# A selective scan in steps of a chunk pair: products of 1024 columns, all products with C on GpSimd, scan result in PSUM

## The chip, the cores and the metric

One core of a Trainium2 chip runs the whole program in one launch. Its engines are TensorE (PE), VectorE (DVE), ScalarE (ACT), GpSimd (POOL) and the queue of SyncE (SP), which issues the transfers. The metric is the device time of one execution in microseconds, from three runs.

## The reference

The input is 16 sequences of 512 positions and 256 channels. A bidirectional selective state-space layer, a residual and a layer norm come first, then a soft mixture of 16 experts with 64 slots each, a residual and a last layer norm. The change touches the scan of the state-space layer alone. For each direction, each of 512 inner channels and each of 16 states n the reference computes, along the positions:

```
dA      = dt * A[n];   dB_u = dt * u * B[n]
dA_cum  = exp(sum of dA over the later positions)
xs      = cumsum(dB_u * dA_cum) / (dA_cum + 1e-12)
y      += xs * C[n]
```

The kernel computes xs as a linear recurrence, s = e * s + g with e = exp(A dt) and g = dt u B, times a guard factor that stands for the 1e-12: (1 + tanh(...)) / 2, with the half folded into C.

## The kernel before, in words

The program has three stages: `sequence_stage` (a loop over the 16 sequences, a prologue and an epilogue), `expert_stage` and `merge_stage`. Only the first is touched.

The 512 inner channels are four chunks of 128 partitions. The scan of a sequence is cut into 128 tiles: two directions, two chunk pairs, 16 states, and the two chunks of the pair (`dir_of`, `chunk_of`, `state_of`). A tile is one state of one chunk, 128 partitions by 512 positions. `TILES` is 128, and a run of 32 tiles (`SEG`) accumulates one pair of chunks of y in PSUM. For a tile t the work is:

- SP (L366, in `load`) broadcasts the rows of B and C for a state to all partitions, into `b_ring` and `c_ring`, three buffers each; one row serves both chunks of a pair.
- ACT (L616, `decay`) writes e into `e_ps`, two banks of PSUM, and (L630) tanh into `f_ps`, two banks of PSUM. e of tile t+1 comes before f of tile t, and must wait for the scan of tile t-1.
- POOL (L504, `inputs`) writes g = dtu * B into `g_ring`, two tiles ahead.
- DVE (L808, `scan`) scans e and g into `s_ring` in SBUF; (L816, `guard`) multiplies (1 + f) by s. For an even tile the result goes back into bank 0 of `f_ps`, and DVE itself multiplies it by C (L825, `times_c`). For an odd tile it goes into `z_ring` in SBUF, and POOL multiplies it by C (L513). Both products go into `v_ring`, six tiles.
- PE (L963) adds v into `y_ps` by a product with the identity, two turns behind; L967 adds the skip term.

DVE's order is: guard(t), scan(t+1), C product of t if t is even. So between a scan and the guard that reads it there is other work, and nothing waits for the instruction just before it.

All engines run the same unrolled 128 tiles per sequence, each in its own program order. Between the tiles each does its share of side work: the projections, convolutions, softplus, norms, softmax over rows and columns and slots of neighbouring sequences. `timetable` and `slot_tiles` fix the tile of each of the side pieces; a piece is filled by PE at its tile and handled by ACT and DVE two to nine tiles later (`side_step`). The two banks of `side` hold the pieces in turn. The two layer norms are split into 15 small steps each, two to a tile, from tile 14 to tile 28 (`norms`, `norm_part`, `norm_step`; the small lines are L64 to L75, the last is L78). Side work on DVE that appears in the rows is L704 (conv gate), L699 (residual gate), L714, L717, L721, L726 and L737 (softplus and the suffix sum of dt), L757 (column softmax), L779 and L785 (copying y out and gating it). POOL also makes dtu = dt * u (L483).

Of the kernel before, what the change touches and what calls it, by code (L numbers as in the profile page):

```python
# [23 lines left out]
P = 128  # L24
# [106 lines left out]
def sequence_stage(nc, xT, x, in_wT, conv_w, conv_b, x_wT, dt_wT, dt_b, A_log, D, out_wT,  # L131
# [28 lines left out]
    TILES = NDIR * PAIRS * SEG  # L160
    assert L == 512 and KI == 4 and KM == 2 and LT == 4 and S == 2 * HS and N == 16
# [13 lines left out]
    VR = 6  # L175


    RING = [i % 3 for i in range(TILES // 2)]
    RING[-1] = 1

# [7 lines left out]
    def dir_of(t):  # L188
        return t // (PAIRS * SEG)
# [4 lines left out]
    with ExitStack() as ctx:  # L194
# [8 lines left out]
        f_ps = ctx.enter_context(nc.psum_tensor("f_ps", [P, 2, 512], F32))  # L203
# [70 lines left out]
        f_ready, g_done, scan_done, z_done = sem("f_ready"), sem("g_done"), sem("scan_done"), sem("z_done")  # L274
        v_even, v_odd, v_used = sem("v_even"), sem("v_odd"), sem("v_used")
# [49 lines left out]
        def _(sp):  # L325
# [25 lines left out]
            def load(at, i, c):  # L351
# [3 lines left out]

                last = max(j for j in range(i - TILES // 2, i) if RING[j % (TILES // 2)] == RING[i])
                if c == 0:
                    sp.wait_ge(g_done, at.b * TILES + (2 * last + 2 + CR))
                else:
                    sp.wait_ge(v_even, at.b * (TILES // 2) + (last + 1 + CR))  # L360
                    sp.wait_ge(v_odd, at.b * (TILES // 2) + (last + 1 + CR))
# [58 lines left out]
            def steps(at, load_next_x):  # L420
                load(at, 0, 0)
                for i in range(TILES // 2):
                    if i + 1 < TILES // 2:
                        load(at, i + 1, 0)
# [47 lines left out]
        def _(pool):  # L472
            make_identity(pool, ident, ident_done)
            pool.sem_inc(v_odd, CR)
# [14 lines left out]
            with pool.Fori(0, B, 1) as b:  # L489
                at = At("loop", b, pool)  # L490
                t0 = pool.snap(b * TILES)
                t0_half = pool.snap(b * (TILES // 2))

                def inputs(t):

                    d, c, i = dir_of(t), chunk_of(t), t // 2
                    if t % (TILES // NDIR) == 0:
                        pool.wait_ge(dtu_done, b * 8 + (d + 1) * KI)
                    k = RING[i]

                    loaded = (b_loaded if t % 2 == 0 else c_loaded)[k]
                    pool.wait_ge(loaded, b * (RING.count(k) * 16) + (RING[:i].count(k) + 1) * 16)
                    pool.wait_ge(scan_done, t0 + (t - 3 + CR))
                    pool.tensor_tensor(g_ring[:, t % 4], dtu[d][:, c], b_ring[:, k], ALU.mult).then_inc(g_done, 1)  # L504

                inputs(0)
                inputs(1)
                for t in range(TILES):
                    if t + 2 < TILES:
                        inputs(t + 2)  # L510
                    if t % 2 == 1:
                        pool.wait_ge(z_done, t0 + (t + 1 + CR))
                        pool.tensor_tensor(v_ring[:, t % VR], z_ring[:, t // 2 % 3], c_ring[:, RING[t // 2]],  # L513
                                           ALU.mult).then_inc(v_odd, 1)
                    for lag in (8, 9):
                        for s in slots_at(t - lag, ("dt0", "dt1")):
                            if TABLE[s][1] % 2 == 1:
                                dtu_of_pair(at, s, (TABLE[s][1] - 9 + lag,))
# [3 lines left out]
        def _(act):  # L522
# [81 lines left out]
            with act.Fori(0, B, 1) as b:  # L604
                at = At("loop", b, act)
                t0 = act.snap(b * TILES)
                t0_half = act.snap(b * (TILES // 2))
                seq4 = act.snap(b * 4)

                def decay(t):  # L610
# [5 lines left out]
                    act.activation(e_ps[:, t % 2], dt[d][:, c], ACT.Exp, scale=a_neg[:, d, c, n:n + 1])  # L616

                decay(0)
                for t in range(TILES):
                    d, c, n = dir_of(t), chunk_of(t), state_of(t)  # L620
                    if t + 1 < TILES:
                        decay(t + 1)
                    if t % (TILES // NDIR) == 0:
                        act.wait_ge(rsum_done, b * 8 + (d + 1) * KI)

                    if t % 2 == 0:
                        act.wait_ge(v_even, t0_half + (t // 2 + CR))
                    else:
                        act.wait_ge(z_done, t0 + (t - 1 + CR))
                    act.activation(f_ps[:, t % 2], rsum[d][:, c], ACT.Tanh,  # L630
                                   scale=a_neg_half[:, d, c, n:n + 1], bias=guard_bias[:]).then_inc(f_ready, 1)
                    for s in range(SLOTS):
                        side_step(at, s, t - tile_of[s])
# [7 lines left out]
        def _(dve):  # L641
# [8 lines left out]
            for sem_, n in ((side_free[0], CR), (side_free[1], CR), (scan_done, CR), (z_done, CR), (v_even, CR),  # L650
# [140 lines left out]
            with dve.Fori(0, B, 1) as b:  # L791
                at = At("loop", b, dve)
                t0 = dve.snap(b * TILES)

# [5 lines left out]
                def scan(t):  # L800

                    flip = (lambda ap: ap) if dir_of(t) == 0 else (lambda ap: ap[:, ::-1])

                    dve.wait_ge(f_ready, t0 + max(t, 1))
                    dve.wait_ge(g_done, t0 + (t + 1 + CR))
                    if t == 0:
                        dve.wait_ge(z_done, t0 + CR)
# [464 lines left out]
```

## Time and profile before

| what | value |
|---|---|
| runs | 7026.24 us median of three (7024.77 to 7026.32) |
| profiled execution, span from first to last instruction | 7017.1 us |
| what the median of the runs has beyond that span | 9.1 us |
| sequence loop within the span | 92.7 to 5934.5 us |
| busy: PE, DVE, ACT, POOL | 78%, 82%, 60%, 60% |
| granted TensorE clock, mean | 0.885 |

For the profiled execution there is no time but its span; the runs were timed by themselves. Busy shares are over the whole span, in which the last 1080 us or so hold no work for POOL. A mean of durations mixes instructions that ran freely with those that were held by something while they ran. The columns of each view are told with its first group of rows below.

### The profile page before, as it was taken

What the parts mean: (1) busy time and instruction counts of PE and PEld (TensorE: products, weight loads), DVE (VectorE), ACT (ScalarE), POOL (GpSimd) and SP (SyncE); (2) the same over time, 40 slices, a digit from 0 to 9 for tenths busy, and PEclk for the clock granted to TensorE, in tenths of its full rate; (3) what the DMA queues carried; (4) which work ended last, traced back from release to release, by engine and by line L of the source; (5) the groups of instructions that cost most, each with busy time, mean ns of one, the idle gap of its engine ahead of it and who ended that gap; (6) DMA issues with size and microseconds to landing.
All of it is one profiled execution on the core that took longest, in us unless ns stands there. A gap on an engine that the chain in (4) does not pass through costs nothing. (4 is left out here: it accounts for less than half of the span.)

```text
span 7017.1 us, 79490 instructions
## 1 busy us (share of the span) xinstructions
PE 5452.5 (78%) x14584; PEld 2611.9 (37%) x14584; DVE 5767.6 (82%) x8375; ACT 4186.0 (60%) x6495; POOL 4206.1 (60%) x3210
## 2 busy tenths in 40 slices
PE   5777777777777777878786877777777777899978
PEld 2333333333333333333333333333333333556566
DVE  7999999989999999999999999999999998222223
ACT  4767676666767676767676767676767665211100
POOL 3767777777777776767676767676777775000000
PEclk8988888888888888889898989898988898999989
DMA  2333333333333333333342423333333332322355
GB/s 76 115 99 113 102 111 102 109 103 107 106 104 105 107 103 110 108 99 116 95 121 90 122 91 119 94 115 99 114 100 112 102 109 79 93 87 87 92 187 203
DMA packets 554755, 755.05 MB, mean 108 GB/s; under 512 B 123584, under 2 KB 272064, under 8 KB 552192
## 3 DMA queue, kind: packets, MB, share of 16 engines
q1 hardware_dynamic: 554240, 750.73, 34.7%
q14 instruction: 503, 4.12, 0.2%
q8 instruction: 12, 0.20, 0.0%
HBM read 660.80 MB, written 89.75 MB: 107 GB/s over the span
## 5 line engine op out<-in xcount | busy, mean ns | idle before, releaser
L963 PE MATMUL y_ps<-v_ring,ident 128*128 128x512 f32 x4096 | 2388.9, 689 | 858.9 <-POOL v_ring L513 304.3
L504 POOL TENSOR_TENSOR g_ring<-dtu,b_ring 128x512 f32<-128x512 f32 x2048 | 2726.3, 1350 | 40.1 <-DMA b_ring<-bc_scr 27.5
L808 DVE TENSOR_TENSOR_SCAN s_ring<-e_ps,g_ring 128x512 f32<-128x512 f32 x2048 | 2478.8, 1210 | 80.8 <-POOL g_ring L504 80.8
L513 POOL TENSOR_TENSOR v_ring<-z_ring,c_ring 128x512 f32<-128x512 f32 x1024 | 1296.1, 1266 | 1599.3 <-DVE z_ring L816 1599.2
L616 ACT ACTIVATE e_ps<-dt,a_neg 128x512 f32<-128x512 f32 x2048 | 1408.7, 688 | 1084.6 <-DVE s_ring L808 1078.6
L630 ACT ACTIVATE f_ps<-rsum,guard_bias,a_neg_half 128x512 f32<-128x512 f32 x2048 | 1572.0, 768 | 30.9 <-DVE z_ring L816 30.3
L963 PEld LDWEIGHTS y_ps<-v_ring,ident 128*128 128x128 f32 x4096 | 775.2, 212 | 2008.9 <-issue 881.3
L816 DVE SCALAR_TENSOR_TENSOR f_ps<-f_ps,s_ring 128x512 f32<-128x512 f32 x1024 | 707.6, 691 | 229.5 <-ACT f_ps L630 186.3
L816 DVE SCALAR_TENSOR_TENSOR z_ring<-f_ps,s_ring 128x512 f32<-128x512 f32 x1024 | 696.1, 680 | 92.3 <-ACT f_ps L630 92.2
L825 DVE TENSOR_TENSOR v_ring<-f_ps,c_ring 128x512 f32<-128x512 f32 x1024 | 679.1, 663 | 0.0
L896 PE MATMUL side<-u,conv_diag 128*128 128x512 f32 x1056 | 489.6, 607 | 41.6 <-ACT disp_ring L597 41.6
L1063 ACT ACTIVATE x_act<-x_gate,x_bg 128x512 f32<-128x512 f32 x128 | 87.9, 687 | 561.6 <-PE x_gate L1095 561.6
L1077 DVE SCALAR_TENSOR_TENSOR x_hT<-x_up,x_bu,x_act 128x512 f32<-128x512 f32 x128 | 96.2, 751 | 373.4 <-PE x_up L1099 373.4
L924 PE MATMUL side<-seT,xnT 128*128 128x512 f32 x544 | 288.8, 659 | 128.6 <-ACT xnT L565 97.6
L944 PE MATMUL side<-dispT_ring,xn 128*128 128x128 f32 x2176 | 299.3, 296 | 67.8 <-ACT dispT_ring L573 67.8
L944 PEld LDWEIGHTS side<-dispT_ring,xn 128*128 128x128 f32 x2176 | 292.5, 211 | 146.9 <-ACT dispT_ring L573 101.2
L896 PEld LDWEIGHTS side<-u,conv_diag 128*128 128x128 f32 x1056 | 203.3, 194 | 309.2 <-issue 254.4
L1207 PE MATMUL m_acc<-m_eo,m_pT 128*128 128x256 f32 x1024 | 240.9, 401 | 64.6 <-DMA m_rinv<-rinv_scr 64.6
L889 PE MATMUL side<-xT_t,w_in 128*128 128x512 f32 x528 | 281.4, 661 | 5.5 <-DVE a_neg L683 4.7
L483 POOL TENSOR_TENSOR dtu<-dt,u 128x512 f32<-128x512 f32 x132 | 233.4, 1769 | 81.2 <-DVE dt L726 81.2
L929 PE MATMUL side<-xnT,seT 128*128 128x512 f32 x544 | 276.4, 635 | 0.0
L1095 PE MATMUL x_gate<-x_xT,x_wg 128*128 128x512 f32 x512 | 242.5, 596 | 16.0 <-DMA x_bu<-in_bu 16.0
(123 smaller groups left out, 5728.4 us busy)
## 6 DMA issues: line engine op xcount, KB each, us to landing
b_ring<-bc_scr SPq DMA_DIRECT2D x1024, 256.0 KB, 3.2
c_ring<-bc_scr SPq DMA_DIRECT2D x1024, 256.0 KB, 3.2
pT_scr<-rowT_ring SPq DMA_DIRECT2D x136, 256.0 KB, 3.6
m_pT<-pT_scr SPq DMA_DIRECT2D x16, 2048.0 KB, 8.3
sT_scr<-sT_ring SPq DMA_DIRECT2D x272, 64.0 KB, 2.4
x_xT<-sT_scr SPq DMA_DIRECT2D x16, 1024.0 KB, 8.9
eo_scr<-x_eo SPq DMA_DIRECT2D x32, 512.0 KB, 5.1
m_eo<-eo_scr SPq DMA_DIRECT2D x16, 1024.0 KB, 10.8
```

Of the source, the lines that this page charges most:

```text
L504: pool.tensor_tensor(g_ring[:, t % 4], dtu[d][:, c], b_ring[:, k], ALU.mult).then_inc(g_done, 1)
L513: pool.tensor_tensor(v_ring[:, t % VR], z_ring[:, t // 2 % 3], c_ring[:, RING[t // 2]], ALU.mult).then_inc(v_odd, 1)
L616: act.activation(e_ps[:, t % 2], dt[d][:, c], ACT.Exp, scale=a_neg[:, d, c, n:n + 1])
L630: act.activation(f_ps[:, t % 2], rsum[d][:, c], ACT.Tanh, scale=a_neg_half[:, d, c, n:n + 1], bias=guard_bias[:]).then_inc(f_ready, 1)
L808: dve.tensor_tensor_scan(flip(s_ring[:, t % 3]), flip(e_ps[:, t % 2]), flip(g_ring[:, t % 4]), 0.0, ALU.mult, ALU.add).then_inc(scan_done, 1)
L816: dve.scalar_tensor_tensor(out=z, in0=f_ps[:, t % 2], scalar=1.0, in1=s_ring[:, t % 3], op0=ALU.add, op1=ALU.mult).then_inc(z_done, 1)
L825: dve.tensor_tensor(v_ring[:, t % VR], f_ps[:, 0], c_ring[:, RING[t // 2]], ALU.mult).then_inc(v_even, 1)
L889: mm = pe.matmul(bank, w_in[:, k, m * P:(m + 1) * P], xT_t[:, k], start=(k == 0), stop=(k == KM - 1))
L896: mm = pe.matmul(bank, conv_diag[:, d, i, k], src[:, i, k:k + L], start=(k == 0), stop=(k == KC - 1))
L924: mm = pe.matmul(bank, xnT[:, k, t * P:(t + 1) * P], seT[:, k, h * HS:(h + 1) * HS], start=(k == 0), stop=(k == KM - 1))
L944: mm = pe.matmul(bank[:, k * P:(k + 1) * P], xn[:, t, k * P:(k + 1) * P], dispT_ring[:, i % 2, t * P:(t + 1) * P], start=(t == 0), stop=(t ...
L963: pe.matmul(y_ps[:, t % 2], ident[:], v_ring[:, t % VR], start=(state_of(t) == 0), stop=True, skip_group_check=True).then_inc(v_used, 1)
```

## The change

What is done by tile becomes done by step, a step being the two tiles of one state of a chunk pair (`STEPS` = 64).

- POOL makes g for both chunks in one product of 1024 columns, the row of B broadcast over the two, into `g_ring` of three pairs, one step ahead. It also makes all products with C, one of 1024 columns a step, into `v_ring` of three pairs. C products on DVE are gone.
- The scan writes into PSUM (`s_ps`, two banks, in the place of `f_ps`); ACT writes tanh into SBUF (`f_ring`, two pairs).
- DVE makes one guard product of 1024 columns a step, into `z_ring` (two pairs in SBUF). Its order is scan(2i), scan(2i+1), guard(i). The guard waits for both scans, and the next scan waits for the guard, since it overwrites `s_ps`.
- ACT's f comes one tile earlier in its order, right behind e of the same tile, with a semaphore of its own for each.
- PE adds v five turns behind (`Y_LAG`) instead of two, and the skip terms go by PE's turn. y is copied out at the fourth tile of a run instead of the second, and gated one tile later.
- The scratch of the program for software-made transfers is set to 1024, which leaves SBUF for the larger rings.

```
-    VR = 6
+    FR, ZR = 2, 2
+    Y_LAG = 5
...
-        f_ps = ctx.enter_context(nc.psum_tensor("f_ps", [P, 2, 512], F32))
+        s_ps = ctx.enter_context(nc.psum_tensor("s_ps", [P, 2, 512], F32))
...
-        g_ring = sb("g_ring", [P, 4, L])
-        s_ring = sb("s_ring", [P, 3, L])
-        z_ring = sb("z_ring", [P, 3, L])
-        v_ring = sb("v_ring", [P, VR, L])
+        g_ring = sb("g_ring", [P, 3, 2, L])
+        f_ring = sb("f_ring", [P, FR, 2, L])
+        z_ring = sb("z_ring", [P, ZR, 2, L])
+        v_ring = sb("v_ring", [P, 3, 2, L])
...
+                def inputs(i):
...
+                    pool.wait_ge(scan_done, t0 + (2 * (before(i) + 1) + CR))
+                    pool.tensor_tensor(g_ring[:, RING[i]], dtu[d][:, pair:pair + 2], both(b_ring[:, k:k + 1]),
+                                       ALU.mult).then_inc(g_done, 1)
+                def times_c(i):
...
+                    pool.wait_ge(z_done, step0 + (i + 1 + CR))
+                    pool.wait_ge(v_used, t0 + (2 * (before(i) + 1) + CR))
+                    pool.tensor_tensor(v_ring[:, RING[i]], z_ring[:, i % ZR], both(c_ring[:, k:k + 1]),
+                                       ALU.mult).then_inc(v_done, 1)
...
+                for i in range(STEPS):
+                    if i + 1 < STEPS:
+                        inputs(i + 1)
+                    times_c(i)
...
+                def guard(t):
...
+                    if t % 2 == 0:
+                        act.wait_ge(z_done, step0 + (i - FR + 1 + CR))
+                    act.activation(f_ring[:, i % FR, t % 2], rsum[d][:, c], ACT.Tanh,
+                                   scale=a_neg_half[:, d, c, n:n + 1], bias=guard_bias[:]).then_inc(f_done, 1)
...
                 def scan(t):
...
+                    dve.wait_ge(e_done, t0 + (t + 1))
+                    if t % 2 == 0:
+                        dve.wait_ge(g_done, step0 + (i + 1 + CR))
+                        dve.wait_ge(z_done, step0 + (i + CR))
+                    dve.tensor_tensor_scan(flip(s_ps[:, t % 2]), flip(e_ps[:, t % 2]), flip(g_ring[:, RING[i], t % 2]), 0.0,
                                            ALU.mult, ALU.add).then_inc(scan_done, 1)
+                def guarded(i):
+
+                    dve.wait_ge(f_done, t0 + (2 * i + 2))
+                    dve.wait_ge(scan_done, t0 + (2 * i + 2 + CR))
+                    dve.wait_ge(v_done, step0 + (i - ZR + 1 + CR))
+                    dve.scalar_tensor_tensor(out=z_ring[:, i % ZR], in0=f_ring[:, i % FR], scalar=1.0, in1=s_ps[:],
                                              op0=ALU.add, op1=ALU.mult).then_inc(z_done, 1)
...
                 for t in range(TILES):
                     part = t // SEG
-                    if t % SEG == 2:
-                        dve.wait_ge(v_used, t0 + (t - 2 + CR))
+                    if t % SEG == 4:
+                        dve.wait_ge(v_used, t0 + (SEG * part + CR))
                         y_out(at, part)
-                    if t % SEG == 3 and part in (0, 3):
+                    if t % SEG == 5 and part in (0, 3):
                         y_gate(at, part)
+                    scan(t)
                     norms(t, 0)
-                    guard(t)
-                    if t + 1 < TILES:
-                        scan(t + 1)
-                    if t % 2 == 0:
-                        times_c(t)
+                    if t % 2 == 1:
+                        guarded(t // 2)
                     norms(t, 1)
...
-                for turn in range(TILES + 2):
-                    t = turn - 2
+                for turn in range(TILES + Y_LAG):
+                    t = turn - Y_LAG
```

## Rows read from the trace of the kernel before

**Rows 1.** Page, part 1: busy us (share of the span) and instructions by engine.

```profile
PE 5452.5 (78%) x14584; PEld 2611.9 (37%) x14584; DVE 5767.6 (82%) x8375; ACT 4186.0 (60%) x6495; POOL 4206.1 (60%) x3210
```

**Rows 2.** Windows: sequence loop; tiles 14-29, 32-39, 68-75 of one sequence.

```profile
core 0: us, PE busy (x) PEld busy (x) DVE busy (x) ACT busy (x) POOL busy (x), PEclk, DMA share, GB/s
92.72:5934.50 5841.78, 4446.09 (x11144) 1956.42 (x11145) 5429.77 (x7442) 4026.24 (x6252) 4195.66 (x3199) 0.87 0.35 106
3046.76:3100.72 53.96, 42.44 (x89) 15.84 (x87) 51.84 (x97) 31.03 (x48) 30.80 (x24) 0.94 0.28 83
3104.95:3128.91 23.96, 14.01 (x28) 5.01 (x27) 22.17 (x29) 17.97 (x25) 15.96 (x12) 0.78 0.33 102
3209.12:3226.06 16.94, 16.89 (x67) 9.56 (x66) 16.52 (x21) 14.94 (x26) 14.95 (x12) 1.00 0.49 149
```

**Rows 3.** Page, part 5: groups of instructions; busy, mean ns, idle before.

```profile
L504 POOL TENSOR_TENSOR g_ring<-dtu,b_ring 128x512 f32<-128x512 f32 x2048 | 2726.3, 1350 | 40.1 <-DMA b_ring<-bc_scr 27.5
...
L816 DVE SCALAR_TENSOR_TENSOR f_ps<-f_ps,s_ring 128x512 f32<-128x512 f32 x1024 | 707.6, 691 | 229.5 <-ACT f_ps L630 186.3
L816 DVE SCALAR_TENSOR_TENSOR z_ring<-f_ps,s_ring 128x512 f32<-128x512 f32 x1024 | 696.1, 680 | 92.3 <-ACT f_ps L630 92.2
L825 DVE TENSOR_TENSOR v_ring<-f_ps,c_ring 128x512 f32<-128x512 f32 x1024 | 679.1, 663 | 0.0
...
L483 POOL TENSOR_TENSOR dtu<-dt,u 128x512 f32<-128x512 f32 x132 | 233.4, 1769 | 81.2 <-DVE dt L726 81.2
```

**Rows 4.** Waits: who waited for whom, total us, times, longest.

```profile
POOL v_ring L513 <- DVE z_ring L816: 1599.2, 974, 4.0
...
DVE f_ps L816 <- ACT f_ps L630: 186.3, 128, 2.0
...
DVE z_ring L816 <- ACT f_ps L630: 92.2, 80, 1.9
```

**Rows 5.** Timeline of DVE in tiles 69 and 70: start, us, line, operation.

```profile
3211.05 1.21 DVE L808 TENSOR_TENSOR_SCAN s_ring<-e_ps,g_ring 128x512 f32<-128x512 f32 x1
3212.18 0.67 DVE L825 TENSOR_TENSOR v_ring<-f_ps,c_ring 128x512 f32<-128x512 f32 x1
3212.76 0.68 DVE L816 SCALAR_TENSOR_TENSOR z_ring<-f_ps,s_ring 128x512 f32<-128x512 f32 x1
3213.36 1.21 DVE L808 TENSOR_TENSOR_SCAN s_ring<-e_ps,g_ring 128x512 f32<-128x512 f32 x1
```

**Rows 6.** One line of the kernel: durations min/median/max in ns.

```profile
L779 DVE TENSOR_TENSOR yg<-y_ps,yg x33: 1199/1199/1224, 98.1 to 5928.7; 128x1024 f32<-128x1024 f32 x33
```

**Rows 7.** Timeline around 3055 us, all engines, in a tile with norm steps.

```profile
3054.64 1.27 POOL L513 TENSOR_TENSOR v_ring<-z_ring,c_ring 128x512 f32<-128x512 f32 x1 [4.00 <-DVE z_ring L816]
...
3055.61 0.33 DVE L66 TENSOR_SCALAR tmp<-mv 128x4 int32<-128x4 int32 x1
...
3055.86 1.27 POOL L504 TENSOR_TENSOR g_ring<-dtu,b_ring 128x512 f32<-128x512 f32 x1
3055.97 1.19 DVE L68 TENSOR_SCALAR rstd<-tmp 128x4 int32<-128x4 int32 x1
```

**Rows 8.** Five lines of DVE with two SBUF operands or more: durations min/median/max.

```profile
L71 DVE SCALAR_TENSOR_TENSOR tmp<-rstd x102: 146/306/1225, 140.3 to 5951.3; 128x4 f32<-128x4 f32 x102
...
L714 DVE TENSOR_SCALAR rsum<-dtu x132: 395/546/1245, 71.8 to 5902.6; 128x512 f32<-128x512 f32 x132
...
L737 DVE TENSOR_TENSOR_SCAN rsum<-one,dt x132: 1210/1366/2215, 77.4 to 5919.1; 128x511 f32<-128x511 f32 x132
...
L757 DVE TENSOR_SCALAR disp_ring<-disp_ring,col_inv x136: 471/576/1423, 240.1 to 6016.4; 128x512 f32<-128x512 f32 x136
...
L704 DVE SCALAR_TENSOR_TENSOR u<-dt,u x132: 675/680/823, 52.7 to 5826.4; 128x512 f32<-128x512 f32 x132
```

**Rows 9.** Timelines of DVE and POOL from 3000.2 us.

```profile
3000.38 2.19 DVE L737 TENSOR_TENSOR_SCAN rsum<-one,dt 128x511 f32<-128x511 f32 x1
...
3001.45 2.17 POOL L504 TENSOR_TENSOR g_ring<-dtu,b_ring 128x512 f32<-128x512 f32 x1
```

**Rows 10.** Timeline of DVE at the start of the ninth sequence.

```profile
3012.48 1.23 DVE L808 TENSOR_TENSOR_SCAN s_ring<-e_ps,g_ring 128x512 f32<-128x512 f32 x1 [5.10 <-POOL g_ring L504]
```

More of the change, by code:

```diff
@@ L173, in sequence_stage, with before @@
     CR = 256
-    VR = 6
-    RING = [i % 3 for i in range(TILES // 2)]
+    FR, ZR = 2, 2
+    Y_LAG = 5
+    RING = [i % 3 for i in range(STEPS)]
     RING[-1] = 1
+    def before(i):
+        return max(j for j in range(i - STEPS, i) if RING[j % STEPS] == RING[i])
     def slots_at(t, kinds):
@@ L354, in load @@
                 ring, loaded = ((b_ring, b_loaded), (c_ring, c_loaded))[c]
-                last = max(j for j in range(i - TILES // 2, i) if RING[j % (TILES // 2)] == RING[i])
+                last = before(i)
                 if c == 0:
-                    sp.wait_ge(g_done, at.b * TILES + (2 * last + 2 + CR))
+                    sp.wait_ge(g_done, at.b * STEPS + (last + 1 + CR))
                 else:
-                    sp.wait_ge(v_even, at.b * (TILES // 2) + (last + 1 + CR))
-                    sp.wait_ge(v_odd, at.b * (TILES // 2) + (last + 1 + CR))
+                    sp.wait_ge(v_done, at.b * STEPS + (last + 1 + CR))
                 if i % (PAIRS * N) == 0 and c == 0:
@@ L506, in _ @@
-                inputs(0)
[L507 to L518, printed above, removed]
+                step0 = pool.snap(b * STEPS)
@@ new lines, in both @@
+                def both(row):
+                    return row.broadcast_to([P, 2, L])
+                def inputs(i):
+                    d, pair, k = dir_of(2 * i), chunk_of(2 * i), RING[i]
+                    if i % (STEPS // NDIR) == 0:
+                        pool.wait_ge(dtu_done, b * 8 + (d + 1) * KI)
+                    pool.wait_ge(b_loaded[k], b * (RING.count(k) * 16) + (RING[:i].count(k) + 1) * 16)
+                    pool.wait_ge(scan_done, t0 + (2 * (before(i) + 1) + CR))
+                    pool.tensor_tensor(g_ring[:, RING[i]], dtu[d][:, pair:pair + 2], both(b_ring[:, k:k + 1]),
+                                       ALU.mult).then_inc(g_done, 1)
@@ L521, in _ @@
+                for i in range(STEPS):
+                    if i + 1 < STEPS:
+                        inputs(i + 1)
+                    times_c(i)
+                    for t in (2 * i, 2 * i + 1):
+                        for lag in (8, 9):
+                            for s in slots_at(t - lag, ("dt0", "dt1")):
+                                if TABLE[s][1] % 2 == 1:
+                                    dtu_of_pair(at, s, (TABLE[s][1] - 9 + lag,))
         @block.scalar
@@ L615, in decay @@
                     act.wait_ge(scan_done, t0 + (t - 1 + CR))
[L616 to L620, printed above, removed]
-                    if t + 1 < TILES:
-                        decay(t + 1)
+                    act.activation(e_ps[:, t % 2], dt[d][:, c], ACT.Exp, scale=a_neg[:, d, c, n:n + 1]).then_inc(e_done, 1)
+                def guard(t):
+                    d, c, n, i = dir_of(t), chunk_of(t), state_of(t), t // 2
                     if t % (TILES // NDIR) == 0:
@@ L626, in _ @@
                     if t % 2 == 0:
[L627 to L631, printed above, removed]
+                        act.wait_ge(z_done, step0 + (i - FR + 1 + CR))
+                    act.activation(f_ring[:, i % FR, t % 2], rsum[d][:, c], ACT.Tanh,
+                                   scale=a_neg_half[:, d, c, n:n + 1], bias=guard_bias[:]).then_inc(f_done, 1)
+                decay(0)
+                guard(0)
+                for t in range(TILES):
+                    if t + 1 < TILES:
+                        decay(t + 1)
+                        guard(t + 1)
                     for s in range(SLOTS):
@@ L649, in _ @@
             dve.memset(y_ps[:], 0.0).then_inc(init_done, 1)
-            for sem_, n in ((side_free[0], CR), (side_free[1], CR), (scan_done, CR), (z_done, CR), (v_even, CR),
+            for sem_, n in ((side_free[0], CR), (side_free[1], CR), (scan_done, CR), (z_done, CR),
                             (x1_done, CR), (xn_normed, CR), (rinv_done, CR)):
@@ L793, in _ @@
                 t0 = dve.snap(b * TILES)
+                step0 = dve.snap(b * STEPS)
                 def norms(t, j):
```

50 lines of the change are left out of this document (13 added, 37 removed).

## The prediction

> **What bounds the kernel now.** I read the page's totals first, then windows, then single instructions. The totals [rows 1] give VectorE (DVE) 82% and GpSimd (POOL) 60%. The sequence loop takes 5841.8 us of the span, or 365.1 per sequence, and in it DVE is busy 93% and POOL 72%; the code after it is not touched [rows 2]. The costliest groups [rows 3] are the scan work. The waits [rows 4] show the order: POOL waits 1599 us for DVE's z, while DVE waits only 186 + 92 = 279 us for ACT's f and hardly for POOL. DVE is the bound.
>
> A step is one state of one chunk pair: two scans, two guards and one C product on DVE, three products on POOL, 64 steps a sequence. In a step without other DVE work starts follow each other by 1.13 us (scan), 0.60 (guard) and 0.58 (C product), because an instruction that waits for nothing starts some 0.08 before the last one ends [rows 5]. That is 2 x 1.13 + 2 x 0.60 + 0.58 = 4.04, and the four steps of tiles 68 to 75 take 16.94 us, 4.24 each [rows 2]. Steps with side work take 6 to 8: the eight with the norms (tiles 14 to 29) take 53.96 together, the four of tiles 32 to 39 take 23.96 [rows 2].
>
> **What the change does to DVE.** The C product goes (0.58). Two guards become one of 1024 columns, which I price from a DVE product of 1024 with one input in PSUM, 1.20 (L779), plus the 0.02 by which the guard exceeds the C product at 512: 1.22 [rows 3, 6]; bounds 1.20 and 2 x 0.69. But the overlap is lost: guard(i) now waits for the scan just before it, and the next scan for guard(i). An instruction that waits for its predecessor starts about 0.035 after it (L66 ends 3055.94, L68 starts 3055.97) [rows 7]. A bare step is 1.13 + 1.21 + 0.035 + 1.22 + 0.035 = 3.63. So DVE is relieved of 0.41 a step, not of 0.66. The scan's output in PSUM I cost at nothing, since the guard into PSUM takes 691 ns against 680 into SBUF [rows 3]; the upper bound is 0.06 each, 0.12 a step, and nothing in these rows allows a gain.
>
> **What it does to POOL.** Per step two products of 1024 columns. No row has this size. Spacing of 512-column products back to back is 1.23 (L513 at 3054.64, L504 at 3055.86) [rows 7], so the upper bound is 2.47. If the fixed share were DVE's (C product 663 ns at 512, 1200 at 1024 [rows 3, 6]), it would be 1.26 x 1.81 = 2.28. I take 2.35, near the middle, and two are 4.70. That alone exceeds the 4.24 of a bare step today: POOL becomes the bound of every step without side work. The order on POOL is g(i+1), v(i), and v(i) waits for z(i), so it can't run ahead more than one step.
>
> The Trainium skill (GPSIMD Engine Reference, Performance versus the Vector engine) gives 4497 ns for a two-input product of 2048 columns. With the 1.26 us of the trace at 512 a line through both gives 2.34 at 1024; the sum would be the same.
>
> **The wait that grows.** Some DVE instructions stretch when POOL is in a product. L71 on four columns takes 146 ns at least and 1225 at most, L737 1210 to 2215, L714 395 to 1245, L757 471 to 1423 [rows 8]. The pair at 3055 shows how: L66 starts while v runs and ends at 3055.94, with v's end (3055.91); g has started at 3055.86, and L68, which waits for L66, ends at 3057.16, with g's end (3057.13) [rows 7]. So the DVE instruction waits until POOL's current product ends, POOL's next one gets in between, and a dependent second instruction waits for a whole product. The other way round POOL loses time too: the product at 3001.45 takes 2.17 while L737 of 1.21 runs its course, so it is held about 0.9, 0.3 less than the instruction's length [rows 9]. All that stretch have two inputs in SBUF, or one input and an output there; scans, guards and C products, with one operand in PSUM, don't.
>
> The Trainium skill (SBUF — State Buffer, Who interferes with whom) says that such a DVE instruction and GpSimd exclude each other for a whole instruction. The trace agrees (L66 and L68 above), and the rule speaks against this change: products twice as long, on an engine that hardly rests, mean longer waits. Without the rule only the faster rival below would stand.
>
> Per sequence there are, by their shortest durations [rows 8]: 8 each of L704 (0.68), L714 (0.40), L737 (1.21), L757 (0.47), and of L717 and L721, taken like L704; 4 of L699, the same; 4 of L726 and 2 of L785, 1024 columns, taken at 1.22 from L779 [rows 6]; 24 small ones of the norms (0.15, as L71) and 8 of L78 (0.40, as L714). Sum 50 us, of which 11 lie in the eight norm steps and 39 in others.
>
> **A step after.** A step begins with scan(2i) when g(i) is there or z(i-1) is done; at that moment v(i-1) starts, too. In a step with such an instruction behind the even scan: it arrives at 1.13, waits until 2.39 (v's end), ends at 2.26 + d, then 1.13 + 0.035 + 1.22 + 0.035: 4.68 + d. POOL has 4.70 + d - 0.3. Behind the guard it delays POOL or DVE by about its length. So 56 steps cost 4.70 each, 263.2, plus their 39 us: 302.2.
>
> Norm steps: in an even tile two dependent small instructions stand side by side. The first ends with v (2.41), POOL's g gets in, the second ends with g (4.74); then scan, guard and two small ones: 7.3. The steps are, with gate and conv instructions (0.6 each), statistics (4 x 0.32 + 0.6) and L78 (4 x 0.32): 6.1, 7.9, 7.9, 10.5, 6.7, 7.9, 7.3, 9.0, together 63.3 against 54.0 now.
>
> Rest: DVE work in PSUM that now finds no gap (row and column maxima, output copies) 5, the eight dtu products of 512 on POOL (1.24 each, half hidden) 4, two places with two such instructions in one tile 3: 12. End of a sequence: 5.1 idle now, until the first g of the next is there [rows 10]; the first g becomes 1.1 longer: 6.2. f in two buffers of a pair takes away DVE's 279 us of waits for ACT, 17 a sequence, which are in today's 365 and not in my sum. TensorE has 16.89 busy in the 16.94 us of tiles 68 to 75, at full granted clock [rows 2]: no spare at 4.24, some at 4.70. Y_LAG 5 gives a filled bank more lead, and v has two steps until its buffer is wanted again; nothing for these, nor for SP, whose loads stay in order and wait for work three steps back.
>
> Sum: 302.2 + 63.3 + 12 + 6.2 = 383.7 per sequence, 18.6 more than 365.1, times 16 is +298. The profiled span 7017.1 becomes 7315; the median of the runs is 9.1 above the span: 7324, say 7325.
>
> **Rivals.** (1) The waits fall into DVE's slack, and POOL's own sum decides: 64 x 4.70 + 10 dtu + 13 held (today (142 + 67) / 16, from the means of L504 and L483 over 1.26 [rows 3]) + 6.2 = 330, or 6470. For it: a bare step leaves DVE 1.07 free, and today the median of L704 is 680 ns against 675 at least [rows 8], so most meet no product. Against it: a wait in an even tile comes between g(i) and z(i), where a step has no second path. It decides as soon as less than two thirds of the 54 by which my sum exceeds this one are paid; at one half it is 357, or 6895. (2) The product of 1024 costs twice that of 512: +0.24 on 56 steps and +0.4 on eight, 16.6 a sequence, 7590. For it: POOL's durations show no fixed share. Against: DVE's do. (3) No change: the product costs 2.28 (-8) and POOL doesn't get in between the small pairs (-10): 365.7, 7035. The pair at 3055 speaks against its second half.
>
> **How the numbers follow.** Forecast 0.55, with its own range 7050 to 7560 (product 2.28 or 2.42, scan into PSUM at its bound, norm steps at 54 or at 70). Rival 1 0.23, rival 2 0.13, rival 3 0.09. Range 6700 to 7640: it cuts off the lower part of rival 1 and little above. 0.2% (14 us) is about what a measurement tells from no change. Faster: rival 1 and a part of 3, 0.25; same 0.05; slower 0.70.
>
> **What would show it.** Right: POOL products near 2.35 and POOL over 85% busy in the loop; plain steps 4.7; L71, L73, L68 up to about 2.4; POOL's waits for z far below 1599; DVE under 90%; the f waits gone. Wrong: plain steps under 4.5, POOL products under 2.2, norm steps under 54, or DVE's short instructions at their shortest durations.

## The result, and the profile after

The changed kernel takes 7193.41 us (median of four runs, 7189.84 to 7197.31) against 7025.51 of the kernel before, run beside it: ratio 1.0241, 95% interval 1.0227 to 1.0256. It is 168 us slower. The forecast was 7325, or 299 slower, with a range of 6700 to 7640: the sign and the mechanism held, the size was too large, and the range was wide enough to hold a gain of 4% as well.

The page of the changed kernel, span and busy times:

```profile
span 7194.4 us, 74433 instructions
...
PE 5485.8 (76%) x14584; PEld 2690.6 (37%) x14584; DVE 5867.7 (82%) x6327; ACT 4217.8 (59%) x6495; POOL 5327.7 (74%) x2186
```

DVE lost 2048 instructions and is busy 100 us longer [rows 1]. Windows of the changed kernel: the sequence loop, and tiles 14 to 29, 32 to 39 and 68 to 75 of one sequence (columns as in [rows 2]):

```profile
core 0: us, PE busy (x) PEld busy (x) DVE busy (x) ACT busy (x) POOL busy (x), PEclk, DMA share, GB/s
96.80:6111.20 6014.40, 4469.15 (x11129) 2031.76 (x11130) 5530.12 (x5394) 4057.05 (x6251) 5316.06 (x2175) 0.84 0.37 103
3140.77:3202.25 61.48, 46.15 (x92) 17.10 (x90) 60.94 (x81) 30.21 (x47) 38.15 (x17) 0.86 0.26 73
3206.93:3230.55 23.62, 10.43 (x21) 4.58 (x21) 23.48 (x23) 17.49 (x24) 22.58 (x9) 0.72 0.32 96
3308.42:3326.65 18.23, 16.14 (x57) 8.99 (x58) 14.25 (x14) 13.99 (x24) 18.19 (x8) 0.91 0.48 140
```

The loop grew from 5841.8 to 6014.4, 10.8 us a sequence. POOL is busy 88% of it instead of 72%. The norm tiles went from 53.96 to 61.48, tiles 32 to 39 stayed (23.96 to 23.62), and tiles 68 to 75 went from 16.94 to 18.23, with POOL busy 18.19 of 18.23 [rows 2]. The groups of the page (busy, mean ns, idle before) that answer to [rows 3]:

```profile
L518 POOL TENSOR_TENSOR v_ring<-z_ring,c_ring 128x1024 f32<-128x1024 f32 x1024 | 2566.9, 2507 | 642.8 <-DVE z_ring L831 616.8
L823 DVE TENSOR_TENSOR_SCAN s_ps<-e_ps,g_ring 128x512 f32<-128x512 f32 x2048 | 2467.6, 1219 | 397.4 <-POOL g_ring L509 338.5
...
L509 POOL TENSOR_TENSOR g_ring<-dtu,b_ring 128x1024 f32<-128x1024 f32 x1024 | 2614.0, 2553 | 47.8 <-DMA b_ring<-bc_scr 45.6
...
L831 DVE SCALAR_TENSOR_TENSOR z_ring<-f_ring,s_ps 128x1024 f32<-128x1024 f32 x1024 | 1249.4, 1220 | 32.7
```

A guard pair takes 1220 ns where the prediction had 1.22, and a scan into PSUM 1219 against 1210 ns. The means of the products, 2507 and 2553, hold waits; their shortest are 2330 and 2332. The waits that answer to [rows 4] (total us, times, longest):

```profile
POOL v_ring L518 <- DVE z_ring L831: 616.8, 560, 4.2
...
DVE s_ps L823 <- POOL g_ring L509: 338.5, 232, 8.9
...
DVE s_ps L823 <- ACT e_ps L628: 36.0, 20, 2.3
```

POOL waits for z 617 us instead of 1599; DVE no longer waits for f, but 339 us for g. New are its 36 us of waits for ACT's e, and within the loop 51 us for TensorE (3 before; the side pieces read at L709 and the copies of y at L791 and L793). How a step without side work runs is seen in two timelines (start, length), first DVE, then POOL, tiles 70 and 71 and the start of 72:

```profile
3312.71 2.35 DVE L823 TENSOR_TENSOR_SCAN s_ps<-e_ps,g_ring 128x512 f32<-128x512 f32 x2 [0.70 <-POOL g_ring L509]
3315.09 1.22 DVE L831 SCALAR_TENSOR_TENSOR z_ring<-f_ring,s_ps 128x1024 f32<-128x1024 f32 x1
3317.35 1.23 DVE L823 TENSOR_TENSOR_SCAN s_ps<-e_ps,g_ring 128x512 f32<-128x512 f32 x1 [1.04 <-POOL g_ring L509]
```

```profile
3312.64 2.35 POOL L518 TENSOR_TENSOR v_ring<-z_ring,c_ring 128x1024 f32<-128x1024 f32 x1
3314.95 2.37 POOL L509 TENSOR_TENSOR g_ring<-dtu,b_ring 128x1024 f32<-128x1024 f32 x1
```

Two scans and the guard end at 3316.31, and DVE then sits idle for 1.04 us until POOL's g is there. POOL starts v at 3312.64 and the next g at 3314.95, 2.31 later, and two such make the step of 4.64: the floor is POOL's pair of products.

Then a step with norm work, tiles 16 and 17, DVE and POOL:

```profile
3146.67 1.23 DVE L823 TENSOR_TENSOR_SCAN s_ps<-e_ps,g_ring 128x512 f32<-128x512 f32 x1
3147.81 1.22 DVE L68 TENSOR_SCALAR rstd<-tmp 128x4 int32<-128x4 int32 x1
3149.06 2.28 DVE L71 SCALAR_TENSOR_TENSOR tmp<-rstd 128x4 f32<-128x4 f32 x1
3151.26 0.68 DVE L718 SCALAR_TENSOR_TENSOR u<-dt,u 128x512 f32<-128x512 f32 x1
3151.86 1.22 DVE L823 TENSOR_TENSOR_SCAN s_ps<-e_ps,g_ring 128x512 f32<-128x512 f32 x1
3152.99 0.14 DVE L73 TENSOR_TENSOR tmp<-tmp,mv 128x4 f32<-128x4 f32 x1
3153.11 1.22 DVE L831 SCALAR_TENSOR_TENSOR z_ring<-f_ring,s_ps 128x1024 f32<-128x1024 f32 x1
3154.25 0.15 DVE L75 SCALAR_TENSOR_TENSOR rstd<-tmp,rstd 128x4 f32<-128x4 f32 x1
3154.43 1.23 DVE L823 TENSOR_TENSOR_SCAN s_ps<-e_ps,g_ring 128x512 f32<-128x512 f32 x1
```

```profile
3146.64 2.35 POOL L518 TENSOR_TENSOR v_ring<-z_ring,c_ring 128x1024 f32<-128x1024 f32 x1 [1.23 <-DVE z_ring L831]
3148.96 2.35 POOL L509 TENSOR_TENSOR g_ring<-dtu,b_ring 128x1024 f32<-128x1024 f32 x1
3154.41 2.35 POOL L518 TENSOR_TENSOR v_ring<-z_ring,c_ring 128x1024 f32<-128x1024 f32 x1 [3.10 <-DVE z_ring L831]
```

L68 stands behind the even scan and ends at 3149.03, when v ends (3148.99). POOL's g has got in at 3148.96, and L71, four columns that need 0.15 us, ends at 3151.34 with it. POOL then waits 3.10 us for z. The step takes 7.76 us, of which 3.2 are these two waits. It is the pair of [rows 7] with products twice as long. The durations (min/median/max) of four such lines, L751 and L771 being L737 and L757 of before [rows 8]:

```profile
L71 DVE SCALAR_TENSOR_TENSOR tmp<-rstd x102: 144/163/2278, 141.1 to 6128.4; 128x4 f32<-128x4 f32 x102
...
L73 DVE TENSOR_TENSOR tmp<-tmp,mv x102: 144/1178/2284, 145.0 to 6128.6; 128x4 f32<-128x4 f32 x102
...
L751 DVE TENSOR_TENSOR_SCAN rsum<-one,dt x132: 1215/1630/2218, 80.3 to 6091.8; 128x511 f32<-128x511 f32 x132
...
L771 DVE TENSOR_SCALAR disp_ring<-disp_ring,col_inv x136: 485/1374/2510, 250.4 to 6191.8; 128x512 f32<-128x512 f32 x136
```

The start of the same sequence on DVE (at [rows 10] the idle time was 5.10), and on POOL:

```profile
3105.63 1.23 DVE L823 TENSOR_TENSOR_SCAN s_ps<-e_ps,g_ring 128x512 f32<-128x512 f32 x1 [8.71 <-POOL g_ring L509]
```

```profile
3103.15 4.66 POOL L509 TENSOR_TENSOR g_ring<-dtu,b_ring 128x1024 f32<-128x1024 f32 x2 [3.82 <-DMA b_ring<-bc_scr]
```

In the kernel before, POOL's wait for the rows of B at this place was shorter:

```profile
3011.10 2.48 POOL L504 TENSOR_TENSOR g_ring<-dtu,b_ring 128x512 f32<-128x512 f32 x2 [2.38 <-DMA b_ring<-bc_scr]
```

### The profile page after: what moved, and what is told of

Its sections match the earlier page's. It is cut to its first block and busy times, and to the rows that moved or that the text cites. A ratio compares the mean times of both kernels' runs of the same rounds, so it can differ in the third digit from the quotient of the medians.

```text
span 7194.4 us, 74433 instructions
## 1 busy us (share of the span) xinstructions
PE 5485.8 (76%) x14584; PEld 2690.6 (37%) x14584; DVE 5867.7 (82%) x6327; ACT 4217.8 (59%) x6495; POOL 5327.7 (74%) x2186
## 5 line engine op out<-in xcount | busy, mean ns | idle before, releaser
L518 POOL TENSOR_TENSOR v_ring<-z_ring,c_ring 128x1024 f32<-128x1024 f32 x1024 | 2566.9, 2507 | 642.8 <-DVE z_ring L831 616.8
L823 DVE TENSOR_TENSOR_SCAN s_ps<-e_ps,g_ring 128x512 f32<-128x512 f32 x2048 | 2467.6, 1219 | 397.4 <-POOL g_ring L509 338.5
L965 PE MATMUL y_ps<-v_ring,ident 128*128 128x512 f32 x4096 | 2327.2, 687 | 491.9 <-POOL v_ring L518 258.5
L509 POOL TENSOR_TENSOR g_ring<-dtu,b_ring 128x1024 f32<-128x1024 f32 x1024 | 2614.0, 2553 | 47.8 <-DMA b_ring<-bc_scr 45.6
L637 ACT ACTIVATE f_ring<-rsum,guard_bias,a_neg_half 128x512 f32<-128x512 f32 x2048 | 1640.3, 801 | 2.1 <-DVE rsum L751 1.3
L965 PEld LDWEIGHTS y_ps<-v_ring,ident 128*128 128x128 f32 x4096 | 831.8, 219 | 1530.2 <-issue 1106.1
L831 DVE SCALAR_TENSOR_TENSOR z_ring<-f_ring,s_ps 128x1024 f32<-128x1024 f32 x1024 | 1249.4, 1220 | 32.7
L938 PE MATMUL side<-ident,row_t 128*128 128x128 f32 x544 | 114.7, 354 | 323.2 <-ACT disp_ring L609 209.4
L910 PE MATMUL side<-xdbl,w_dt 16*128 16x512 f32 x264 | 177.4, 757 | 192.4 <-ACT disp_ring L609 152.7
L905 PE MATMUL side<-u,w_x 128*48 128x512 f32 x264 | 189.4, 886 | 176.2 <-DVE u L718 176.2
```

The costliest lines, as they stand in the source:

```text
L509: pool.tensor_tensor(g_ring[:, RING[i]], dtu[d][:, pair:pair + 2], both(b_ring[:, k:k + 1]), ALU.mult).then_inc(g_done, 1)
L518: pool.tensor_tensor(v_ring[:, RING[i]], z_ring[:, i % ZR], both(c_ring[:, k:k + 1]), ALU.mult).then_inc(v_done, 1)
L637: act.activation(f_ring[:, i % FR, t % 2], rsum[d][:, c], ACT.Tanh, scale=a_neg_half[:, d, c, n:n + 1], bias=guard_bias[:]).then_inc(f_don ...
L823: dve.tensor_tensor_scan(flip(s_ps[:, t % 2]), flip(e_ps[:, t % 2]), flip(g_ring[:, RING[i], t % 2]), 0.0, ALU.mult, ALU.add).then_inc(sca ...
L831: dve.scalar_tensor_tensor(out=z_ring[:, i % ZR], in0=f_ring[:, i % FR], scalar=1.0, in1=s_ps[:], op0=ALU.add, op1=ALU.mult).then_inc(z_do ...
L965: pe.matmul(y_ps[:, t % 2], ident[:], v_ring[:, RING[t // 2], t % 2], start=(state_of(t) == 0), stop=True, skip_group_check=True).then_inc ...
```

## The experiments

Times are medians, each with its ratio to the kernel before, run beside it on the same chip, and the 95% interval. The kernel before took 7021.8 to 7025.5 beside the others. The other columns are us of a mean sequence, from the distances between starts of even scans in the trace, averaged over fifteen sequences: a bare step (mean of the three of tiles 70 to 75), the 55 steps that are neither norm steps nor the last, the eight norm steps (tiles 14 to 29), and the last. In the four kernels with 4.37, two of the three bare steps take 4.25 and the third 4.60.

| kernel | us | ratio (interval) | bare step | 55 steps | norm | last | sum |
|---|---|---|---|---|---|---|---|
| before | 7025.5 | 1 | 4.24 | 301.9 | 53.5 | 9.5 | 364.9 |
| changed | 7193.4 | 1.0241 (1.0227 to 1.0256) | 4.64 | 302.6 | 61.5 | 11.7 | 375.7 |
| products halved | 7187.0 | 1.0240 (1.0219 to 1.0260) | 4.92 | 313.3 | 50.8 | 11.5 | 375.7 |
| changed, no small norm steps | 6973.9 | 0.9935 (0.9918 to 0.9952) | 4.64 | 302.7 | 47.7 | 11.5 | 361.9 |
| before, no small norm steps | 6884.9 | 0.9808 (0.9792 to 0.9825) | 4.24 | 302.2 | 44.5 | 9.5 | 356.3 |
| before, scan in PSUM | 7034.5 | 1.0017 (1.0007 to 1.0026) | 4.37 | 302.9 | 53.3 | 9.6 | 365.8 |
| that, g of 1024 | 7189.0 | 1.0238 (1.0221 to 1.0255) | 4.37 | 304.1 | 59.7 | 11.5 | 375.4 |
| before, all C on GpSimd | 7185.2 | 1.0234 (1.0217 to 1.0251) | 4.92 | 306.6 | 57.9 | 10.4 | 375.0 |
| scan in PSUM, f early | 6808.0 | 0.9696 (0.9679 to 0.9712) | 4.37 | 290.1 | 51.9 | 9.7 | 351.8 |
| changed, f late | 7329.4 | 1.0439 (1.0423 to 1.0455) | 4.96 | 310.8 | 61.9 | 11.4 | 384.2 |
| before, norm steps in fours | 6963.3 | 0.9917 (0.9900 to 0.9933) | 4.24 | 302.2 | 49.7 | 9.5 | 361.4 |
| changed, norm steps in fours | 7136.6 | 1.0161 (1.0146 to 1.0177) | 4.66 | 303.3 | 57.3 | 11.8 | 372.3 |
| scan in PSUM, f early, norms in fours | 6751.5 | 0.9615 (0.9602 to 0.9628) | 4.37 | 290.2 | 48.3 | 9.6 | 348.1 |

**Products halved** (changed kernel).

```
-                    pool.tensor_tensor(v_ring[:, RING[i]], z_ring[:, i % ZR], both(c_ring[:, k:k + 1]),
-                                       ALU.mult).then_inc(v_done, 1)
+                    for q in range(2):
+                        ins = pool.tensor_tensor(v_ring[:, RING[i], q], z_ring[:, i % ZR, q], c_ring[:, k], ALU.mult)
+                    ins.then_inc(v_done, 1)
```

and likewise for g. 

> The changed kernel with each GpSimd product of 1024 columns as two of 512, nothing else. Theory (two costs: GpSimd's own sum, and waits as long as its product): steps without side work become 4 x 1.23 = 4.93 us instead of 4.65, some 6 us more a sequence over 21 of them; the norm steps, where a dependent small instruction waits a whole product, fall from 61.5 to about 50; together about 7160 us (7080 to 7220), and the longest durations of L71 and L73 fall from 2.28 to about 1.2. Rival (the length of the waits is hidden, only GpSimd's sum counts): 64 x 0.28 = 18 us a sequence more, 7480 us.

Measured 7187.0, the time of the changed kernel. A bare step is 4.92, and the norm steps fell by 10.7 us a sequence to 50.8, as the theory had it, and the longest L73 (min/median/max) is a short product's length:

```profile
L73 DVE TENSOR_TENSOR tmp<-tmp,mv x102: 143/155/1170, 140.3 to 6120.3; 128x4 f32<-128x4 f32 x102
```

The 55 other steps rose by 10.7, more than the 6 expected. So the product of 1024 columns buys POOL a shorter sum and pays it back in the norm steps. Part of the rise is no matter of POOL's sum. Where POOL runs product behind product without a pause, a DVE instruction isn't always let in after the current one:

```profile
2478.99 6.53 DVE L730 TENSOR_SCALAR rsum<-dtu 128x512 f32<-128x512 f32 x1
```

```profile
2479.10 1.26 POOL L510 TENSOR_TENSOR g_ring<-dtu,b_ring 128x512 f32<-128x512 f32 x1
2480.32 2.47 POOL L520 TENSOR_TENSOR v_ring<-z_ring,c_ring 128x512 f32<-128x512 f32 x2
2482.76 2.47 POOL L510 TENSOR_TENSOR g_ring<-dtu,b_ring 128x512 f32<-128x512 f32 x2
```

L730, which needs 0.41, started before these five products and ended after them. That happened to L730 once, but a conv gate (L720) took 4.3 instead of 0.67 once in nearly every sequence.

**The small norm steps left out**, in the changed kernel and in the one before (same edit).

```
+                if at.mode == "loop" and 2 <= k % NORM_STEPS < NORM_STEPS - 1:
+                    dve.sem_inc(chain, 1)
+                    return
```

In both, `rstd` is set to 1 once at the start, so the norms of the loop are not computed.

> The changed kernel without the small instructions of the norms in the loop (L64 to L75; the reciprocal root is left at 1, so the norms are not computed). Theory (waits behind GpSimd's products): the eight norm steps fall from 61.5 to about 46 us, 250 us in all, 6945 us, though the instructions left out are only 24 x 0.15 = 3.6 us a sequence. Rival (GpSimd's sum bounds these steps too): at most 2 us a sequence, 7160 us.

> The kernel before without the same small instructions (norms not computed). Theory: their waits are half as long there, so the norm steps fall from 53.5 to about 45, 6890 us, and the distance between the changed kernel and this one shrinks from 168 to about 50 us. Rival: the distance stays near 168 us.

Measured 6973.9 and 6884.9. Leaving out instructions that need 24 x 0.15 = 3.6 us a sequence saves 13.8 in the changed kernel and 8.6 in the one before, nearly all in the norm steps (61.5 to 47.7, 53.5 to 44.5). The distance of the two kernels shrinks from 168 to 89 us; I had expected 50. The small norm steps are about half of the loss.

**Scan in PSUM alone** (kernel before; guards of even tiles stay in place in `s_ps`).

```
-                    dve.scalar_tensor_tensor(out=z, in0=f_ps[:, t % 2], scalar=1.0, in1=s_ring[:, t % 3],
+                    dve.scalar_tensor_tensor(out=z, in0=f_ring[:, t % 3], scalar=1.0, in1=s_ps[:, t % 2],
```

> The kernel before with one part of the change alone: the scan writes into PSUM (two banks), ACT writes tanh into three SBUF buffers, even guards stay in place in PSUM; order, 512 columns, and C products divided between DVE and GpSimd as before. Theory: DVE's 279 us of waits for ACT's f go and the scan into PSUM costs nothing: 6760 to 6850 us. Rival 1: the waits come back as waits for something else, 7026 us. Rival 2: the scan is slower into PSUM by 0.06 us, 123 us more on DVE's path.

Measured 7034.5, 0.17% slower. The scan into PSUM costs next to nothing: 1.224 us against 1.214 in a bare step. The gain did not come. The time is that of rival 1, but not for its reason: the waits of [rows 4] did not turn into others, those for ACT's f itself are still there (L818 is the guard).

```profile
DVE s_ps L818 <- ACT f_ring L627: 194.6, 128, 3.4
...
DVE z_ring L818 <- ACT f_ring L627: 87.2, 80, 1.8
```

**And g as one product of 1024** (on the kernel just told; C products stay divided).

```
-                    pool.tensor_tensor(g_ring[:, t % 4], dtu[d][:, c], b_ring[:, k], ALU.mult).then_inc(g_done, 1)
+                    pool.tensor_tensor(g_ring[:, i % 2], dtu[d][:, c:c + 2], b_ring[:, k:k + 1].broadcast_to([P, 2, L]),
+                                       ALU.mult).then_inc(g_done, 2)
```

> The kernel before with the scan in PSUM, as run before, and g made as one product of 1024 columns for the pair; C products stay divided. GpSimd has 2.33 + 1.23 = 3.56 us a step, below DVE's 4.04, so only the length of the wait behind a product differs from the run before. Theory (waits grow with the product): 40 to 120 us more than the 7034 us there, longest L71 and L73 about 2.3 us. Rival (length is hidden while GpSimd isn't the bound): 7034 us or some 10 us less, for half the issues.

Measured 7189.0: 155 us lost, more than the theory's upper end, in a kernel in which POOL has 3.56 us of work a step. Norm steps took 6.4 us a sequence, the last step 1.9, the others 1.2; bare steps stayed as they were, 4.37. This edit changes little but the length of one product, and the longest L73 shows it:

```profile
L73 DVE TENSOR_TENSOR tmp<-tmp,mv x102: 141/164/2311, 142.9 to 6116.7; 128x4 f32<-128x4 f32 x102
```

The 6.4 us in the norm steps, 102 of the 155 in all, are this. The rest is less clear: the edit also gives g two pair buffers for four single ones, and the whole pair now waits for the rows of C, which only the odd g did before. POOL's waits for rows rose from 39 to 104 us, and DVE's for g from 83 to 139, half of it at the start of a sequence.

**All products with C on GpSimd alone** (kernel before, 512 columns).

```
-                    if t % 2 == 0:
-                        times_c(t)
...
-                        pool.tensor_tensor(v_ring[:, t % VR], z_ring[:, t // 2 % 3], c_ring[:, RING[t // 2]],
+                    pool.tensor_tensor(v_ring[:, t % VR], z_ring[:, t % 4], c_ring[:, RING[t // 2]],
```

> The kernel before with one part of the change alone: all products with C on GpSimd, still tile by tile with 512 columns, f in PSUM as before, z of every tile in SBUF. GpSimd then has four products of 1.23 a step, 4.93 us, DVE 3.46. Theory (GpSimd's sum is the floor of steps without side work): plain steps go from 4.24 to 4.93, the lighter DVE gains nothing, and the time comes near that of the changed kernel with halved products: 7150 us (7100 to 7230). Rival (GpSimd has room, its share was 72% in the loop): DVE's 0.58 a step is gained in the steps with side work and the time falls below 7026 us.

Measured 7185.2, inside the expected 7100 to 7230, and a bare step is 4.92 instead of 4.24, POOL's four products of 1.23. That is the floor. Outside the bare steps DVE has more to wait for than before: f (324.6 us against 279), g (179.7 against 81), and the products themselves, as in the kernel with halves (L710, 0.40 at its shortest, took up to 4.02).

```profile
DVE z_ring L813 <- ACT f_ps L626: 324.6, 290, 3.5
...
DVE s_ring L804 <- POOL g_ring L503: 179.7, 223, 6.1
```

**f early** (scan in PSUM, and ACT's order as in the changed kernel, with a semaphore of its own for e).

```
                 decay(0)
+                guard(0)
                 for t in range(TILES):
                     if t + 1 < TILES:
                         decay(t + 1)
+                        guard(t + 1)
```

> The kernel before with the scan in PSUM, as run before, and ACT's f of tile t+1 right behind its e, as the changed kernel has it, with a semaphore of its own for e. The run before left DVE's 282 us of waits for f where they were, so the buffers were not their cause. Theory: ACT's order is the cause, f comes too late behind ACT's side work; the waits go and the time is 6760 to 6880 us. Rival: they come back as waits for e, and the time stays at 7034 us.

Measured 6808.0, 226 us less than the same kernel with f late; 12.8 of its 14.0 us a sequence lie outside the norm steps. The waits for f are gone, and almost none for e stand in their place (L815 is the scan):

```profile
DVE s_ps L815 <- POOL g_ring L505: 105.7, 50, 5.9
...
DVE s_ps L815 <- ACT e_ps L617: 26.2, 50, 0.9
```

**f late in the changed kernel** (the same lines the other way round).

> The changed kernel with ACT's order put back: f of tile t behind e of tile t+1. The kernel before gained 226 us from the earlier f, so the change must hold a gain of this kind if DVE needs f in time there, too. Theory: the guard of a pair is one instruction and waits for the f of its odd tile, which now comes behind the next e; DVE waits again for f, and the time is 7250 to 7400 us; a gain was hidden in the change. Rival: the pair step leaves DVE 1 us free, which takes up the late f, and the time stays near 7193 us; then the earlier f brought nothing in this form.

Measured 7329.4: 136 us more, and the guard waits for f again.

```profile
DVE z_ring L830 <- ACT f_ring L637: 330.5, 432, 3.7
```

So the change holds a gain of 136 us from ACT's order, and without it would have cost 308 (the kernel before took 7021.8 beside it).

**Norm steps in fours.** In the kernel before behind the even C product, in the changed one between the odd scan and the guard.

```
-                    norms(t, 0)
...
-                    norms(t, 1)
+                    if t % 2 == 0:
+                        for j in range(4):
+                            norms(t, j)
```

> The kernel before with its four small norm steps of two tiles all behind DVE's C product of the even tile, where GpSimd has mostly run out of work and waits for z, and none at the odd tile. Theory (the waits behind GpSimd's products are what the norms cost): the waits of L64 to L75 go from about 130 us to under 40, the norm steps from 53.5 to about 46 a sequence, 6900 us. Rival (their cost is the chain of dependent instructions): 7026 us or more, since four dependent ones now stand in a row.

> The changed kernel with the four small norm steps of two tiles all between the odd scan and the guard, none behind the even scan. Theory: only the first waits, until GpSimd's g ends, and then GpSimd has nothing to do until z; the norm steps go from 61.5 to about 54 a sequence, 7075 us. Rival: GpSimd's own sum or the chain of four sets these steps, 7190 us.

Measured 6963.3 and 7136.6: gains of 60 and 57 us, half of what was expected in each. The timeline of DVE in the kernel before so edited shows why (the same norm steps as in [rows 7], L68 to L75):

```profile
3029.84 0.67 DVE L825 TENSOR_TENSOR v_ring<-f_ps,c_ring 128x512 f32<-128x512 f32 x1
3030.42 0.28 DVE L68 TENSOR_SCALAR rstd<-tmp 128x4 int32<-128x4 int32 x1
3030.74 0.17 DVE L71 SCALAR_TENSOR_TENSOR tmp<-rstd 128x4 f32<-128x4 f32 x1
3030.94 0.16 DVE L73 TENSOR_TENSOR tmp<-tmp,mv 128x4 f32<-128x4 f32 x1
3031.13 0.16 DVE L75 SCALAR_TENSOR_TENSOR rstd<-tmp,rstd 128x4 f32<-128x4 f32 x1
3031.21 0.69 DVE L704 SCALAR_TENSOR_TENSOR u<-dt,u 128x512 f32<-128x512 f32 x1
```

None of the small ones waits for a whole product any more (L68 takes 0.28 instead of 1.19, and none more than 0.30), but four dependent ones start 0.32, 0.20 and 0.19 us apart, and together take 0.8. Measured from each start to the next start on DVE, the 24 small instructions take 5.9 us a sequence in the kernel before so edited, and took 11.6: the waits are gone, but the expected 46 would have needed some 4. Another 1.1 us went to the scans: with no norm step between them, the even guard stands directly behind its scan six times more in a sequence, and starts 0.10 after it instead of 0.08 before its end. In the changed kernel the small ones fell from 22.3 to 14.9, but the six gates (L713, L718) in these steps took 4.2 us more: the waits for products moved to them.

**Both gains together** (scan in PSUM, f early, norm steps in fours).

> The kernel before with the scan in PSUM, ACT's f early, and the norm steps in fours: the two gains found, together. If they are independent, 6808 - 60 = 6750 us (6730 to 6775), below both kernels. Rival: the early f already filled the same gaps of DVE, and 6808 us stays.

Measured 6751.5 (five runs, 6749.8 to 6754.1), ratio 0.9615: 3.9% faster than the kernel before and 6.1% faster than the changed one. The two gains add up: norm steps in fours bring 56.5 here and 59.8 alone. It keeps 512-column products and the divided C products; POOL is busy 62% of the span, DVE 84%.

## Why the prediction was right, and where its size was off

**DVE's step.** 3.63 us was nearly right: the two scans start 1.13 apart, the guard starts 0.03 after the second and takes 1.22. But the next scan starts at least 0.10 after the guard, not 0.035, which makes 3.70. The step before was mispriced in the same way. Its starts add up to 4.04 in the prediction, and it takes 4.24, because an even guard has its own scan directly in front of it; the words ahead of the prediction, that nothing waits for the instruction just before it, are true of odd guards alone. It starts 0.11 after that scan's end instead of 0.08 before it:

```profile
3209.12 1.21 DVE L808 TENSOR_TENSOR_SCAN s_ring<-e_ps,g_ring 128x512 f32<-128x512 f32 x1
3210.44 0.70 DVE L816 SCALAR_TENSOR_TENSOR f_ps<-f_ps,s_ring 128x512 f32<-128x512 f32 x1
```

So DVE is relieved of 0.54 and not of 0.41, still less than the C product's 0.58. As POOL's 4.64 bounds the bare step, neither error reached the sum.

**POOL's product.** I took 2.35; the spacing is 2.32 and the shortest duration 2.33. POOL bounds bare steps, 4.64 against the 4.70 said. Rival 2 (twice the cost) would need 2.46. The Trainium skill's 4497 ns (GPSIMD Engine Reference, Performance versus the Vector engine) is for an addition of 2048 columns, where the prediction says product; the estimate drawn from it, 2.34, agrees with the trace.

**The growing wait.** The longest L71 went from 1225 to 2278 ns, as said (L68's stayed at 1219: it is the first of its pair and waits only for the rest of v). The eight norm steps were forecast step by step as 63.3; they are 61.5. The halved products (61.5 to 50.8) and the g of 1024 (53.3 to 59.7) show that the product's length makes the difference, and the left out norm steps that it is paid at these instructions. Summed over DVE's instructions in the loop, the time by which they exceed the shortest of their line is 203 us before and 867 in the changed kernel (an estimate from the trace's durations); the difference is four times the loss, so most of it fell where DVE had time to spare. Rival 1, that the waits fall into slack, would have been 330 a sequence; 375.7 is 85% of the way from there to my 383.7.

**What was mis-sized.** My 383.7 against 375.7 a sequence is 8 us, 128 in all. Norm steps account for 1.8 of it, the last step for -0.8 (10.9 said, 11.7 measured). The rest, 6.9, lies in the 55 other steps: 55 x 4.70 + 39 + 12 = 309.5 said, 302.6 measured. Of it, 55 x 0.06 = 3.3 is POOL's 4.70 for 4.64; the other 3.6 must be in the 12 us for dtu products, maxima and output copies, which in part did find gaps, or in the 39. Which, was not tried. Against it stand waits that the sum had at nothing: DVE's 51 us for TensorE in the loop, 3 a sequence, and 36 for ACT's e. TensorE's granted clock was 0.857 in the changed kernel and 0.885 in the one before, and 0.91 against 1.00 in tiles 68 to 75; whether the lower clock is behind these waits, no run separates.

**What was wrong in the reasons.** I put the end of DVE's waits for f down to f's two pair buffers. The kernel with three buffers and the old order kept them (282 us), the one with f directly behind its e lost them, and the changed kernel with the old order has them again: the cause is ACT's order. I also expected DVE below 90% in the loop; it is 92%, and an instruction held behind a product counts as busy. And I said nothing of the last step being longer by more than the first g: DVE idles 8.71 there instead of 5.10, 3.6 more. The longer last v and first g explain 2.2 (two times 2.33 - 1.23), and POOL's wait between them for the rows of B, 3.82 instead of 2.38, the other 1.4. Over fifteen sequences the idle time is 8.07 instead of 5.20, and that wait has 0.7 of the 2.9. Why the rows come later was not tried.

**Where the 168 us come from.** Three parts were run on the kernel before, two of them with the scan in PSUM, and they don't add: g of 1024 costs 155, all C products on GpSimd 162, the early f gives 226 there and 136 in the changed kernel. With f late the changed kernel loses 308, near the sum of the first two, 317; then ACT's order gives back 136. That this is more than chance is not shown: DVE's new order with the paired guard, and `Y_LAG`, were not run alone. The Trainium skill (SBUF — State Buffer, Who interferes with whom) says of DVE's 2-port modes that whoever issues first has the ports shared with GpSimd for the whole instruction, and that two SBUF inputs contend with GpSimd, too. The runs agree on the whole instruction, and they add its price for a DVE instruction of four columns that meets a product: up to 1.23 us in all with 512 columns, 2.28 with 1024. They don't agree on who comes first: L730 of the kernel with halves started before five products that passed it, and the measurement decides.

## What to carry to other kernels

When DVE has short instructions that exclude GpSimd, keep GpSimd's instructions short, leave it pauses (with products back to back one DVE instruction was held 6.1 us by products of 1.23), put DVE's short ones where GpSimd waits for DVE, and count the waits by place, not by mean. Moving work to the engine with the lower busy share helps only if its own sum per step stays below the bound: 60% busy over the span was 3.74 of 4.24 us in bare steps [rows 2]. It isn't enough: with g of 1024 alone GpSimd's sum was 3.56, and 155 us were lost. And when a change has several parts, run them one by one: here one part, a swap of two ACT instructions, was worth 136 to 226 us (with tanh in SBUF), and the others hid it.

## What the runs showed of the hardware that was not expected

- A product on GpSimd has a small fixed share: starts are 1.23 us apart at 512 columns and 2.32 at 1024, so 0.14 is fixed, if the rest grows with the columns.
- A DVE instruction that has what it reads directly in front of it starts after it by 0.03 us in one place (guard behind scan in the changed kernel, 911 times) and by 0.10 in others (guard behind scan in the kernel before, 432 times, and at the least scan behind guard in the changed one). What makes the difference stays open.
- A DVE instruction held by GpSimd isn't always let in after the current product: with products back to back, five more passed one (L730 above).
- Three kernels with quite different divisions of work (products halved, g of 1024 alone, all C on GpSimd alone) came out at 7185 to 7189 us. Their parts differ (norm steps 50.8, 59.7, 57.9; bare steps 4.92, 4.37, 4.92), so nothing points to a common bound.
- ACT's tanh takes 801 ns into SBUF and 768 into PSUM; what that costs was not tried by itself; the scan into PSUM and tanh into SBUF together cost 10 us.
